# Scaled expert rows leave PSUM by pairs of tiles, and come back in runs of four on two queues

## The reference

```python
h = _layernorm(x) * (1 + cb) + sb
tokens = h.reshape(2048, 128)
gates = softmax(tokens @ wg)                      # 8 experts
idx1, idx2 = the two largest; g1, g2 = their gates / (sum of both)
f1, f2 = slot of the token in expert idx1, idx2   # 512 slots for each expert
disp[f1] += tokens; disp[f2] += tokens
eo = gelu(disp @ w_gate[e]) @ w_down[e]           # for each expert e
ffn = g1 * eo[f1] + g2 * eo[f2]                   # weights are 0 beyond an expert's 512 slots
out = x + gb * ffn                                # gb: one row of 128 for each sequence
```

## Time and profile before

| | us |
|---|---|
| median of 3 runs | 373.05 |
| lowest and highest run | 373.0, 373.94 |
| the profiled execution: its own time | 374.51 |
| the profiled execution: span from first to last instruction | 372.5 |

### The profile page before, as it was taken

One profiled execution on the slowest core, in us unless ns is written; L12 is line 12 of the kernel. 1 busy time (PEld: TensorE's weight loads), 2 busy tenths in 40 slices (PEclk: granted clock), 3 DMA queues, 4 the chain that ended last, 5 costly groups with the idle time before them and its releaser, 6 DMA issues.

```text
span 372.5 us, 4896 instructions
## 1 busy us (share of the span) xinstructions
PE 275.3 (74%) x1586; PEld 214.7 (58%) x1586; DVE 233.6 (63%) x694; ACT 148.1 (40%) x278; POOL 127.1 (34%) x149
## 2 busy tenths in 40 slices
PE   1847557849599899998999899994303899999400
PEld 1423233426567577776887798884202589989400
DVE  2469999969869879598577726749450432342116
ACT  3650452447724457153463636450200454351100
POOL 3101270264100230313020472153748116466733
PEclk9996976976899999999999999999555599999955
DMA  7993003000200000000000010000104634211175
GB/s 221 405 387 161 1 1 114 0 0 0 91 24 2 0 1 3 1 2 0 2 0 1 2 52 7 4 29 31 43 30 131 172 96 129 66 35 44 55 198 147
DMA packets 18312, 25.01 MB, mean 67 GB/s; under 512 B 2032, under 2 KB 14448, under 8 KB 17520
## 3 DMA queue, kind: packets, MB, share of 16 engines
q1 hardware_dynamic: 16240, 20.46, 16.9%
q0 software_dynamic: 2048, 4.25, 3.4%
HBM read 15.16 MB, written 11.68 MB: 72 GB/s over the span
## 4 chain that ended last, share of the span: by engine, by line
PE 50%; DVE 26%; issue 7%; ACT 6%; DMA 5%; POOL 4%; SPq 1%; DVEq 0%; ACTq 0%; POOLq 0%
PE ps L1202 46%; DVE nd L850 3%; DVE qp L838 3%; DVE kv L829 2%; PE ps L1223 2%; POOL line L399 2%; DVE acc L927 2%; DMA wmod_sb<-in_wmod 1%; ACT hid L579 1%; DMA wide<-chosen 1%; DVE st L715 1%; DMA phi<-line 1%; PE ps L1466 1%; POOL rstd L365 1%; DVE phi L811 1%
## 5 line engine op out<-in xcount | busy, mean ns | idle before, releaser
L1202 PE MATMUL ps<-w_sb,hid 128*128 128x128 f32 x512 | 59.9, 276 | 0.7 <-DVE acc L927 0.7
L1202 PEld LDWEIGHTS ps<-w_sb,hid 128*128 128x128 f32 x512 | 58.7, 192 | 1.9 <-DVE acc L927 0.9
L579 ACT ACTIVATE hid<-ps,s_sb 128x512 f32<-128x512 f32 x64 | 43.1, 684 | 27.7 <-PE ps L1202 26.9
L1202 PE MATMUL ps<-kv,c_sb 128*128 128x512 f32 (+1 forms) x96 | 41.7, 547 | 6.0 <-DVE qp L838 5.0
L399 POOL DMA_INDIRECT line<-h3r,dest_i x32 | 31.3, 978 | 23.3 <-DVE dest_i L1045 14.6
L1202 PE MATMUL ps<-h2h,w1h 128*128 128x512 f32 x80 | 37.1, 463 | 0.5 <-ACT hid L579 0.3
L1202 PE MATMUL ps<-h2l,w1h 128*128 128x512 f32 x80 | 32.4, 405 | 0.0
L1202 PE MATMUL ps<-h2h,w1l 128*128 128x512 f32 x80 | 32.2, 403 | 0.0
L1202 PEld LDWEIGHTS ps<-wd_sb,hid 128*128 128x128 f32 x256 | 29.7, 192 | 0.8 <-ACT hid L270 0.2
L1202 PE MATMUL ps<-wd_sb,hid 128*128 128x128 f32 x256 | 30.0, 275 | 0.0
L1202 PEld LDWEIGHTS ps<-kv,c_sb 128*128 128x128 f32 x96 | 18.3, 213 | 18.7 <-issue 17.0
(11 more groups left out here) (199 smaller groups left out, 530.7 us busy)
## 6 DMA issues: line engine op xcount, KB each, us to landing
line<-wuh SPq DMA_DIRECT2D x8, 262.0 KB, 13.3
line<-line SPq DMA_DIRECT2D x8, 262.0 KB, 3.2
phi<-line SPq DMA_DIRECT2D x8, 262.0 KB, 3.1
wd_sb<-in_w_down SPq DMA_DIRECT2D x1, 2048.0 KB, 12.3
chosen<-wuh SPq DMA_DIRECT2D x4, 512.0 KB, 11.3
wst<-in_w_up SPq DMA_DIRECT2D x2, 1024.0 KB, 5.6
wide<-chosen SPq DMA_DIRECT2D x8, 256.0 KB, 4.6
x_sb<-in_x SPq DMA_DIRECT2D x4, 256.0 KB, 6.9
```

The lines of the kernel that those rows point to most:

```text
L579: a_.activation(hid[:, e % 2, u % FC, :], ps[:, B_UP[u % 2], :], ACT.Silu, bias=s_sb[:, c:c + 1]).then_inc(hid_ready, 1)
L1202: return m.matmul(o, l, r, start=start, stop=stop)
```

## The change

Five edits go together.

1. The down products of experts 0 to 6 always use banks 6 and 7, two tiles in each. PE signals after each pair of tiles, DVE waits for a pair and evicts it. The waits on `edown_ps` count twice as far. Expert 7 uses banks 6, 7, 0, 1.
2. The eviction multiplies by the row's weight and by the gate row in one instruction with two operands (`scalar_tensor_tensor` for `tensor_scalar`). As one tile can hold tokens of both sequences, a gate tile is built first for each tile of an expert (`row_gates`: four `scalar_tensor_tensor` of 128 x 128 for each expert, into the free tiles `conv` and `diff`), from `in_first`, which says whether a row's token belongs to the first sequence (one more small instruction in `row_addresses`).
3. The token number (`C_TOK`) becomes block, partition, tile: a partition's four tiles of a block are neighbours in `chosen`, 2048 bytes in a run.
4. The load back is split: SP loads the first choices (four DMAs), ACT, after its last gelu, the second choices (four DMAs). Each block and half has its own semaphore.
5. POOL's four additions and DVE's multiplication by the gate row are gone; DVE adds both halves to the residual, two additions a block.

```diff
--- before.py
+++ after.py
@@ -162,10 +162,14 @@
         second = sb("second", [P, E2, BT])
         trash = sb("trash", [P, E2, BT])
         addr = sb("addr", [P, 4, BT])
+        in_first = sb("in_first", [P, E2, BT])
         row_w = sb("row_w", [P, E2, BT])
         back_i = sb("back_i", [P, E2, BT], U32)
 
         back = wide[:, 0:TILES * 2 * D].rearrange("p (k t d) -> p k t d", t=TILES, k=2)
+
+        def gate_rows(e):
+            return (conv if e % 2 == 0 else diff)[:].rearrange("p (t d) -> p t d", t=BT)
 
         def rows(e):
             return phi[:, e % 2].rearrange("p t d -> p (t d)")[:, 0:BT * ROW].rearrange("p (t d) -> p t d", t=BT)
@@ -208,15 +212,15 @@
             sem(n) for n in ("rowsT_ps", "rowsT_hi", "rowsT_lo", "eup_ps", "ehid_ready", "edown_ps", "eout_ready",
                              "back_i_ready"))
         chosen_written = [sem(f"chosen_written_{i}") for i in range(2)]
-        back_in = L("back_in")
-        both_ready, comb_ready, stored = sem("both_ready"), sem("comb_ready"), sem("stored")
+        back_in = [L(f"back_in{k}") for k in range(2)]
+        comb_ready, stored = sem("comb_ready"), sem("stored")
 
 
 
         LAG = BT + 3
         STEPS = NBLK * E1 + LAG
         LAST = NBLK - 1
-        LAST_BANKS = (7, 0, 1, 2)
+        LAST_BANKS = (6, 7, 0, 1)
 
 
 
@@ -264,10 +268,19 @@
                 u = e * FC + c
                 act.wait_ge(eup_ps, u + 1)
                 if e >= 2 and c == 0:
-                    act.wait_ge(edown_ps, e - 1)
+                    act.wait_ge(edown_ps, 2 * (e - 1))
                 if e < 2 and c == 0:
                     act.wait_ge(down_ps, NBLK * E1)
                 nc.scalar.activation(hid[:, e % 2, c, :], ps[:, 2 + c, :], ACT.Gelu).then_inc(ehid_ready, 1)
+
+        def load_back(engine, k):
+
+            for half in chosen_written:
+                engine.wait_ge(half, 16 * BT * E2 // 2)
+            cv = chosen[0:2 * TOKENS, :].rearrange("(k b p t) d -> p k b (t d)", k=2, b=NBLK, p=P)
+            for b in range(NBLK):
+                engine.dma_start(tiles(back[:, k], b).rearrange("p t d -> p (t d)"), cv[:, k, b]) \
+                    .then_inc(back_in[k][b], 16)
 
         block = ctx.enter_context(nc.Block())
 
@@ -323,12 +336,7 @@
                 sp.dma_start(rows(e), line1[e * LINE1:e * LINE1 + CAP, :].rearrange("(t p) d -> p t d", p=P)) \
                     .then_inc(rows_in[e], 16)
 
-            cv = chosen[0:2 * TOKENS, :].rearrange("(k t p) d -> p k t d", k=2, p=P)
-            for half in chosen_written:
-                sp.wait_ge(half, 16 * BT * E2 // 2)
-            for b in range(NBLK):
-                for k in range(2):
-                    sp.dma_start(tiles(back[:, k], b), tiles(cv[:, k], b)).then_inc(back_in[b], 16)
+            load_back(sp, 0)
             for b in range(NBLK):
                 sp.wait_ge(comb_ready, b + 1)
                 sp.dma_start(tiles(ov, b), tiles(x_sb, b)).then_inc(stored, 16)
@@ -438,11 +446,6 @@
                     pool.wait_ge(eout_ready, BT * e + j + 1)
                     g.indirect_dma_start(out=chosen, out_offset=bass.IndirectOffsetOnAxis(back_i[:, e, j:j + 1], 0),
                                          in_=xstage(e)[:, j, :], in_offset=None).then_inc(chosen_written[e % 2], 16)
-
-            for blk in range(NBLK):
-                pool.wait_ge(back_in[blk], 32)
-                a, b_ = tiles(back[:, 0], blk), tiles(back[:, 1], blk)
-                g.tensor_tensor(a, a, b_, ALU.add).then_inc(both_ready, 1)
 
 
         @block.scalar
@@ -688,6 +691,7 @@
                 if e >= 1:
                     gelus(act, e - 1)
             gelus(act, E2 - 1)
+            load_back(a_, 1)
 
         @block.vector
         def _(dve):
@@ -1065,6 +1069,7 @@
                 dve.wait_ge(rows_in[e], 16)
                 number, w_first, w_diff = (rows(e)[:, :, D + i] for i in range(3))
                 step(v.scalar_tensor_tensor(addr[:, 0, :], second[:, e, :], float(TOKENS), number, ALU.mult, ALU.add))
+                v.tensor_scalar(in_first[:, e, :], number, float(SEQ), None, ALU.is_le)
                 step(v.scalar_tensor_tensor(addr[:, 1, :], number, 0.0, trash[:, e, :], ALU.is_equal, ALU.mult))
                 step(v.tensor_tensor(addr[:, 2, :], second[:, e, :], w_diff, ALU.mult))
                 after()
@@ -1150,6 +1155,8 @@
             route_c(LAST)
             counts()
             slot_kinds()
+            step(v.tensor_tensor(gtmp[:, 0, 0, :], modb[:, 0, 3, :], modb[:, 1, 3, :], ALU.subtract))
+            after()
 
 
             def low_part(e):
@@ -1159,31 +1166,44 @@
                 v.tensor_tensor(h2l[:, e % 2, :], ps[:, e % 2, :], h2h[:, e % 2, :].bitcast(F32), ALU.subtract) \
                     .then_inc(rowsT_lo, 1)
 
+            def row_gates(e):
+                if e >= 2:
+                    dve.wait_ge(eout_ready, BT * (e - 1))
+                for j in range(BT):
+                    last = v.scalar_tensor_tensor(gate_rows(e)[:, j, :], gtmp[:, 0, 0, :], in_first[:, e, j:j + 1],
+                                                  modb[:, 1, 3, :], ALU.mult, ALU.add)
+                step(last)
+
             for e in range(2):
                 row_addresses(e)
                 low_part(e)
+                row_gates(e)
             for e in range(E2):
                 if e + 2 < E2:
                     row_addresses(e + 2)
                     low_part(e + 2)
-                if e < E2 - 1:
-                    dve.wait_ge(edown_ps, e + 1)
+                after()
                 if e >= 2:
                     dve.wait_ge(chosen_written[e % 2], 16 * BT * (e // 2))
                 for j in range(BT):
-                    bank = 6 + e % 2
+                    bank = 6 + j // 2
                     if e == E2 - 1:
                         bank = LAST_BANKS[j]
-                        dve.wait_ge(edown_ps, e + 1 + j)
-                    v.tensor_scalar(xstage(e)[:, j, :], ps[:, bank, j * D:(j + 1) * D], row_w[:, e, j:j + 1],
-                                    None, ALU.mult).then_inc(eout_ready, 1)
+                        dve.wait_ge(edown_ps, 2 * e + 1 + j)
+                    elif j % 2 == 0:
+                        dve.wait_ge(edown_ps, 2 * e + 1 + j // 2)
+                    v.scalar_tensor_tensor(xstage(e)[:, j, :], ps[:, bank, j * D:(j + 1) * D], row_w[:, e, j:j + 1],
+                                           gate_rows(e)[:, j, :], ALU.mult, ALU.mult).then_inc(eout_ready, 1)
+                if e + 2 < E2:
+                    row_gates(e + 2)
 
             for blk in range(NBLK):
-                a = tiles(back[:, 0], blk)
-                dve.wait_ge(both_ready, blk + 1)
-                step(v.tensor_tensor(a, a, modb[:, blk // BPB, 3, None, :].broadcast_to([P, BT, D]), ALU.mult))
-                after()
-                v.tensor_tensor(tiles(x_sb, blk), tiles(x_sb, blk), a, ALU.add).then_inc(comb_ready, 1)
+                xb = tiles(x_sb, blk)
+                dve.wait_ge(back_in[0][blk], 16)
+                step(v.tensor_tensor(xb, xb, tiles(back[:, 0], blk), ALU.add))
+                after()
+                dve.wait_ge(back_in[1][blk], 16)
+                v.tensor_tensor(xb, xb, tiles(back[:, 1], blk), ALU.add).then_inc(comb_ready, 1)
 
 
         @block.tensor
@@ -1489,8 +1509,12 @@
                 if e + 1 < E2 - 1:
                     expert_up(e + 1)
                 if e < E2 - 1:
-                    claim(6 + e % 2, eout_ready, BT * (e + 1))
-                    down(6 + e % 2, wd_sb[:, e], hid[:, e % 2], edown_ps, ehid_ready, e * FC)
+                    for j in range(BT):
+                        if j % 2 == 0:
+                            claim(6 + j // 2, eout_ready, BT * e + j + 2)
+                        last = down_tile(6 + j // 2, j, wd_sb[:, e], hid[:, e % 2], ehid_ready, e * FC)
+                        if j % 2 == 1:
+                            last.then_inc(edown_ps, 1)
             expert_up(E2 - 1)
             for j in range(BT):
                 claim(LAST_BANKS[j], eout_ready, BT * (E2 - 1) + j + 1)
@@ -1533,7 +1557,8 @@
     const[:, C_COS:C_COS + TPB * DH] = cos.reshape(P, -1)
     const[:, C_SIN:C_SIN + TPB * DH] = sin.reshape(P, -1)
     const[:, C_REV:C_REV + E2] = E2 - np.arange(E2)
-    const[:, C_TOK:C_TOK + TILES] = np.arange(TILES) * P + i[:, None] + 1
+    t = np.arange(TILES)
+    const[:, C_TOK:C_TOK + TILES] = t // BT * W + i[:, None] * BT + t % BT + 1
     const[:, C_SLOT:C_SLOT + BT] = np.arange(BT) * P + i[:, None]
     const[:, C_TRASH:] = 2 * TOKENS + 1 + np.arange(E2 * BT) * P + i[:, None]
     cmask = np.stack([i[:, None] < i, np.ones((P, P), bool)], axis=1).astype(ml_dtypes.bfloat16)
```

## The result

The changed kernel takes 367.63 us (median of 4 runs, 366.98 to 368.72), the kernel before 373.3 beside it; the ratio is 0.9836, with a 95% interval of 0.9803 to 0.987: 1.6% faster. The profiled execution takes 368.22, its span is 366.4 (372.5 before).

A forecast was written before the change was run, and what follows sets the result against it. PE bounds until expert 5, then POOL's run of twelve scatters, then the load back and additions. Gains of 1.87 and 4.4 to 4.6 us, in sum 6.3 to 6.4, take 373.05 to about 366.7; range 365.5 to 369.4.

The forecast's parts named there:

- Pairs of tiles: Expert stage: evicting down products by pairs starts expert 5's first scatter, and POOL's last twelve, earlier; gain 1.87 us.
- Gates hidden on DVE: Expert stage: four gate tiles per expert, 1.14 us together, fit DVE's idle time; cost 0 on the path.
- The slack that I named, that of the low part: DVE's low part of expert 3 was ready 4.4 us before PE needed it; about 4.2 less addresses.
- the rival: Expert stage: POOL locks out DVE's gate tiles, 5.0 us per expert instead of 1.14; time 373.5 to 375; chance 0.05.
- the lock: Expert stage: each of DVE's four gate tiles would wait for a whole POOL scatter, 1.26 us.
- Way back: Last scatter's landing to DVE's last addition: 9.4 us instead of 13.8, gain 4.4 to 4.6.
- the early first pair: Load back: with both queues issuing at once, first pair there 3.4 us after first issue, 3.85 less 0.43.
- The rate: Load back: runs of 2048 bytes move at 377 GB/s instead of 284, 1.39 us a block.
- The rival made of the rule: Load back: rate stays that of short pieces, pairs 2.1 us apart; time 368.6 to 369.4; chance 0.14.
- The last store: End of the kernel: the store stays at 2.97 us after the last addition, 2.3 of it the landing.

The follow-up runs named there:

- A: Not a run: part of each profiled span up to the start of expert 2's transposes on PE; 297.90 us before, 298.57 changed.
- C: Not a run: span part from the landing of the last scatter to DVE's last addition; 13.84 us before, 9.01 changed.
- B: Not a run: span part from the start of expert 2's transposes to the landing of the last scatter; 57.79 us before, 56.12 changed.

## Why the prediction was right

The median was forecast at 366.7 and came out at 367.63; the ratio is a gain of 6.1 against 6.4 forecast. Without A, which the edits hardly touch, the edits gained 6.8 in the profiled executions, 0.4 more than forecast; that the spans differ by only 6.1 is due to A, 0.67 later in the changed kernel's first execution. Step by step:

- *Pairs of tiles*: right in mechanism, 1.87 forecast, 1.67 to 1.8 measured. The half of 3.73 was too much: the first pair was evicted 2.10 after the start of the products (335.84 to 337.94), the second 1.67 later. So halving a run of PE put its first results too early.
- *Gates hidden on DVE*: right. Four take 1.15, DVE has 3.75 of 6.80, PE waits for nothing. The slack that I named, that of the low part, was not where the rival decides: with more work the evictions come late first (by 1.56 at a turn of 6.88), and PE takes DVE's pace once DVE's whole turn is clearly past 6.80 (7.62). The rival also had the lock the wrong way round: with gates built four times it was POOL that was held, while DVE's twelve kept 3.23.
- *Way back*: 9.4 forecast, 8.97 to 9.33 measured. The first addition came 3.2 after the last landing instead of 3.45, but the reason given for the early first pair was wrong. The forecast took 0.43 off because two queues issue at once. With one queue the first block was ready no later (3.52 after the landing), and with short runs on two queues the first addition began 356.66 - 352.78 = 3.88 after it, as in the kernel before (359.60 - 355.69 = 3.91). It is the longer runs that brought it forward; that 3.45 came so near was luck. The rate was 367 against 377; and DVE needs 1.34 per block (357.90 to 359.24), not 1.42, since an addition that does not wait for the one before it follows it by 0.60. ACT issues its loads at 0.36 to 0.45 each, like SP.
- *Where the gain of the way back lies*: from the single runs, 1.6 to 1.9 the runs of 2048 bytes, 0.2 to 0.6 the second queue, 1.6 to 2.0 the additions off POOL. Both transfer edits, about 2.1, and the additions, about 1.9, make 4.0 of the 4.83 in C; no run split the remaining 0.8, and the gate row in the eviction was not tried alone. The multiplication is a candidate: in the kernel before it stood between POOL's last addition and DVE's, which end 2.60 apart, and without it 1.15. As the old way back took 13.84 once and 14.86 once, the size of the remainder is uncertain too.
- *The second queue*: the rule that it saves only issue time (the Trainium skill, DMA: Bandwidth & Descriptors, section Issuing engines are not separate DMA queues) would fit the 0.2 to 0.6 in C, one issue or so, but the one execution with a single queue and long runs does not bear it out: its first block came no later, and its loads moved 302 GB/s instead of 367 at the same share. The measurement decides here, for what one execution is worth. The rival made of the rule fell: the rate did not stay at 284, and for 367 it took the long runs and the second queue together.
- *The last store*: forecast unchanged; it ended 0.25 sooner in every kernel in which DVE alone adds. The store itself did not change; before, POOL's closing DRAIN ended the program 0.2 after SP was through, and without POOL's additions it is over long before.

## What to carry to other kernels

Where a queue of equal transfers ends a stage, find the one that started its last unbroken run, and make that one earlier; anything behind it is free until the run meets another engine. A return through DRAM is worth laying out for the reader: the writer, here scattered rows at its own pace, did not notice. Before giving an idle engine more work, add up its whole turn against the engine that sets the pace: with a turn of 7.62 DVE gave PE a pace of 7.63, and already at 6.88 late evictions and held scatters cost 4.3 us in B. An engine that closes slowly should not work last: here POOL's final additions held the end of the program after every result was stored.

## What the runs showed of the hardware

- Full DMA engines, reading from DRAM, moved 287 GB/s in pieces of 512 bytes on two queues, 367 in pieces of 2048 on two queues, and 302 in pieces of 2048 on one queue. The last scatter landed 2.22 to 2.24 us after its start in all twelve executions, whether the rows of neighbouring tokens stood side by side or 2048 bytes apart.
- A run of sixteen DVE instructions with two SBUF operands held an indirect scatter of POOL until the run was over, for up to 3.11 us instead of 0.96, but only one scatter of four; a run of twelve one-operand sums held none. The Trainium skill, SBUF — State Buffer, section Who interferes with whom, says that a DVE instruction with two SBUF inputs contends with one of GpSimd that reads SBUF, and that the contention is an exclusive lock. The hold here outlasted a single instruction (0.27) by far, and why three scatters of four escape I could not settle.
- POOL's closing DRAIN ended 5.3 us after POOL's last instruction, an addition or a scatter, and the program did not end before it.
